# A two-block transformer step on one core: order of work in the mixture's first batch, at the seam between mixture and scan, and in SP's queue

## The chip, the cores and the metric

The kernel runs on one core of a Trainium2 chip. The metric is the device time of one execution in microseconds. Engines: TensorE (PE; its loads of stationary data are PEld), VectorE (DVE), ScalarE (ACT), GpSimd (POOL) and SyncE (SP), which issues most DMA transfers.

## The reference, cut to what matters

Two blocks, each with a token mixer and a feed-forward part, on x of shape (2, 2048, 256). The change touches the feed-forward part of the first block (a soft mixture of experts) and the mixer of the second (a state-space scan).

```python
# block 0, feed-forward: soft mixture, e=8 experts with t=128 slots each
logits = einsum('bsd,etd->bset', xn, se)
dispatch = softmax(logits, axis=1)                 # over the tokens
slots = einsum('bsd,bset->betd', xn, dispatch)
processed = gelu(slots @ w1) @ w2
combine = softmax(logits.reshape(b, s, e*t), -1)   # over the slots
x = x + gb * einsum('bnd,bsn->bsd', processed, combine)
# block 1, mixer: state space, 8 heads
h = layernorm(x) * (1 + ca) + sa
zxbcdt = layer_norm(h) @ W_in + b_in               # z, xs, B, C, dt
h_t = exp(dt*A) * h_(t-1) + (dt*xs) (x) B ;  y_t = h_t . C_t + D*xs
x = x + ga * (h + (y * silu(z)) @ W_out + b_out)
```

## The kernel before, in words

Each engine has a queue of its own, written out by hand, and waits on semaphores. `soft_mixture` and `state_space` are two such programs, one after the other; between them all engines meet at a barrier and the semaphores are cleared (`recycle`).

**The mixture** treats the batches b = 0 and 1 one after the other. `raw[e]` keeps the logits of expert e for 2048 tokens (128 slots x 2048). The combining softmax needs each token's largest logit. `spread_tops` sends these maxima through DRAM and back to all partitions (`top`). Then VectorE subtracts them (`shift`, L1268, 128x2048), ScalarE takes the exponential in place (`weights`, L1614), and TensorE multiplies with the experts' outputs (`combine`, L1846). The outputs are made by `outputs(b, et)` on TensorE: in batch 0 it takes 24 products of 128x256 an expert (three products of split operands for each of 8 parts, L61 to L63) into one of two PSUM banks, `pO[:, et % 2]`. `processed(b, e)` (VectorE, L1272) multiplies the result with the gate and frees the bank; `outputs` of expert et waits for `processed` of et - 2. The experts go in two halves of ES = 4. Between them TensorE makes `hidden(b, 1, j)`, ScalarE `gelu` (L1610) and the rounded `hidden_high` (L1586), and VectorE `hidden_low` (L1195). ScalarE has two `weights` ahead of the second half's `gelu`s and six behind them. `last_vector` is seven small VectorE operations on row statistics.

VectorE's order at the end of batch 0: for e in 0..3 `shift(e)`, `processed(e)`; then `shift(4)`, two `hidden_low`, `shift(5)`, six `hidden_low`, `shift(6)`, `shift(7)`; `last_vector`; `processed(4)` to `processed(7)`; then `modulate` for batch 1 and the loop of 16 `update(t)` behind `combine(t)`.

**The seam.** While batch 1 is combined, pairs of row tiles (PAIRS = 8 in each batch) are already normalised for the scan: `state_rows`, `state_offset` (VectorE), `state_normed`, `state_turned` (ScalarE), `state_turn`, `state_steps` (TensorE), `step_sizes` (VectorE, L1341), `turned_out` (SP, L1031). A pair's residual is x += ga * (h + b_out), three operations of 128x512. GpSimd makes these for most pairs (L1132 to L1136), VectorE for the last three of batch 1 (`residual`, L1423 to L1429), at the very end of its queue, ahead of the last `step_sizes`.

**The scan** has 32 steps n (batch n % 2, tile n // 2). Step n on TensorE: `project(n + 1)` (18 products of 128x384; the second third waits for `gate_bias`), `turn_y(n - 1)`, `states(n)`, `state_rows(n + 1)`, `within(n)`, `correlate(n + 1)`, `outputs(n - 1)`. ScalarE: `high`, `evacuate(n + 1)`, `y_high(n - 1)`, `by_state(n + 1)`, `decay(n + 1)`: eight Relus of 128x128 (L2234), then the copy of the next projection's bias into PSUM (`gate_bias`, L2217), then an exponential (L2239). VectorE: `weigh(n)` (L2358), `low(n + 2)`, `initial(n)` (L2363, L2365), `y_low(n - 1)` (L2369), `update(n)` (L2376), `gates(n + 1)` (L2347), `sums(n)` (L2382), `masked(n + 1)` (L2352), `finish(n - 1)` (L2387). GpSimd: `products` (L2144, L2146), `add_skip`, `skip` (with `dskip`), `gate`. `gate_bias(n)` writes the bank that `gates(n - 1)` reads, so it waits for it.

SP sends what a step needs just ahead (`stage(n)`: `cs`, `etot` and the 512 KB of `cumb`, L2098 to L2100), each `stage` once step n - 2 has read the buffers. The last 14 tiles' decays are made in the scan's first steps (`late_ratio`, `late_sizes`, `late_cumulate`, `late_sums`, `late_kept`, `late_turned`) and go through DRAM; `stage(5)` waits for that. `inputs(k)` loads a quarter of the projections' input (1024 KB). `m.wg`, `m.wu` and `m.wd` are weights that are first read at step 23.

## Time and profile before

| | |
|---|---|
| timed runs (3) | median 1670.1 us, 1668.47 to 1670.71 |
| profiled execution | 1671.12 us, its span 1669.4 us |
| granted TensorE clock over the span | 0.985 of full speed |
| busy: TensorE, VectorE, ScalarE, GpSimd | 1580.2 (95%), 1187.8 (71%), 776.2 (46%), 575.1 (34%) us |
| the mixture's batch 0 tail | about 497 to 541 us |
| seam between mixture and scan | about 866 to 871 us |
| scan | 871 to about 1200 us |

The span runs from the first to the last instruction. A busy share says how long an engine worked, not what held the end back; for that one reads, in each stretch, which wait ends last. The granted clock is that of TensorE alone: 1.00 is 2.4 GHz, 0.50 is 1.2 GHz.

### The profile page before, as it was taken

To read this page: it belongs to the slowest core of one execution; us is meant where nothing else is said; L and a number is where in the kernel's file an instruction comes from. 1 tells how busy PE (TensorE), PEld (TensorE's weight loads), DVE (VectorE), ACT (ScalarE), POOL (GpSimd) and SP (SyncE) were. 2 spreads that over 40 slices of the span, in tenths; PEclk is the share of its full clock that TensorE was granted. 3 is DMA by queue.
4 is the path that set the end of the run, shared out by engine and by line. 5 is a ranking of instruction groups with operands and counts; after the bars stand their busy time and mean duration, and the time that the engine had idled before them with its cause. 6 is when DMAs were issued, how large, how long until landed. Compare 5 with 4: busy or idle time off the path is not lost. (4 is left out here: it accounts for less than half of the span.)

```text
span 1669.4 us, 25600 instructions
## 1 busy us (share of the span) xinstructions
PE 1580.2 (95%) x9192; PEld 1365.4 (82%) x9192; DVE 1187.8 (71%) x2656; ACT 776.2 (46%) x1554; POOL 575.1 (34%) x474
## 2 busy tenths in 40 slices
PE   6899989999998999999979999999899999999996
PEld 4689878988888888867867889988688778888895
DVE  6877688864467756656877899989777736666763
ACT  3333333353356134427247778778411315444542
POOL 2100020000000003320536778877400024777764
PEclk9999999999999999999989999999899999999999
DMA  7000000010021000222025322322142135565643
GB/s 233 5 1 1 1 1 1 1 51 1 1 67 36 9 5 19 79 71 84 28 72 185 86 79 81 95 81 79 65 140 63 39 87 158 137 175 137 159 109 38
DMA packets 80886, 115.28 MB, mean 69 GB/s; under 512 B 15693, under 2 KB 60281, under 8 KB 80121
## 3 DMA queue, kind: packets, MB, share of 16 engines
q1 hardware_dynamic: 66808, 95.16, 17.9%
q0 software_dynamic: 12288, 17.31, 5.8%
q8 instruction: 74, 1.21, 0.3%
q10 hardware_dynamic: 1664, 1.18, 0.2%
q14 instruction: 52, 0.42, 0.1%
HBM read 85.32 MB, written 27.68 MB: 68 GB/s over the span
## 5 line engine op out<-in xcount | busy, mean ns | idle before, releaser
L2015 POOL DMA_INDIRECT k_xe<-rows_dram,idx x64 | 82.4, 1288 | 179.4 <-DVE idx L3087 141.1
L3154 POOL DMA_INDIRECT out<-k_eo,idx x64 | 117.0, 1828 | 74.5 <-DVE k_eo L3250 57.3
L1846 PE MATMUL d_pO<-d_sp,d_raw 128*128 128x257 f32 x512 | 114.6, 380 | 3.3 <-DVE x L1280 3.2
L1846 PEld LDWEIGHTS d_pO<-d_sp,d_raw 128*128 128x128 f32 x512 | 95.6, 189 | 17.7 <-DVE x L1280 4.1
L576 ACT ACTIVATE b_p<-b_pS,b_nmax 128x384 f32<-128x384 f32 (+16 forms) x32 | 38.1, 1192 | 131.7 <-DVE b_nmax L718 131.7
L61 PE MATMUL b_pO<-b_vh,b_ph 128*128 128x256 f32 x302 | 87.6, 290 | 7.3 <-DVE b_pl L699 7.2
L62 PE MATMUL b_pO<-b_vh,b_pl 128*128 128x256 f32 x302 | 85.3, 283 | 0.0
L63 PE MATMUL b_pO<-b_vl,b_ph 128*128 128x256 f32 x302 | 85.3, 283 | 0.0
L366 POOL TENSOR_TENSOR x<-x,b_vrow 128x256 f32<-128x256 f32 x32 | 24.1, 785 | 168.5 <-DVE b_hs L645 168.4
L2234 ACT ACTIVATE g_dlm<-d_cumb,mod 128x128 f32<-128x128 f32 x256 | 78.6, 400 | 2.0 <-DMA d_cumb<-cum_dram 2.0
L3209 ACT ACTIVATE k_act_g<-k_pg 128x512 f32<-128x512 f32 x64 | 38.3, 598 | 87.2 <-PE k_pu L63 87.0
L3267 DVE TENSOR_TENSOR k_hid<-k_act_g,k_pu 128x512 f32<-128x512 f32 x64 | 44.0, 687 | 42.8 <-ACT k_act_g L3209 42.2
L1599 ACT COPY d_raw<-pL 128x512 f32<-128x512 f32 x64 | 37.4, 587 | 79.6 <-PE pL L63 79.6
L61 PE MATMUL k_po<-k_wh,k_hh 128*128 128x256 f32 x256 | 72.4, 283 | 0.6 <-issue 0.6
L63 PE MATMUL k_po<-k_wl,k_hh 128*128 128x256 f32 x256 | 72.5, 283 | 0.0
L62 PE MATMUL k_po<-k_wh,k_hl 128*128 128x256 f32 x256 | 72.4, 283 | 0.0
L2845 ACT ACTIVATE i_act_g<-i_pg 128x512 f32<-128x512 f32 x30 | 17.9, 598 | 114.7 <-PE i_pu L63 114.7
L69 PE MATMUL pL<-d_winh,g_uh 128*128 128x384 f32 x186 | 65.1, 350 | 3.4 <-ACT pL L2217 2.6
L61 PE MATMUL b_pS<-b_kh,b_qh 128*128 128x512 f32 (+5 forms) x172 | 65.6, 381 | 1.4 <-DVE b_vl L691 1.4
L61 PEld LDWEIGHTS b_pO<-b_vh,b_ph 128*128 128x128 f32 x302 | 57.6, 191 | 10.8 <-DVE b_pl L699 10.5
L699 DVE TENSOR_TENSOR b_pl<-b_pT,b_ph 128x512 fp32r<-128x512 f32 (+3 forms) x86 | 49.9, 617 | 23.2 <-ACT b_ph L566 23.2
L1147 POOL MEMSET d_sp<- 128x4 f32 x4 | 0.3, 105 | 189.8 <-PE pL L63 165.8
(570 smaller groups left out, 5432.2 us busy)
## 6 DMA issues: line engine op xcount, KB each, us to landing
d_cumb<-cum_dram SPq DMA_DIRECT2D x32, 512.0 KB, 4.3
k_wf<-in_WgT SPq DMA_DIRECT2D x16, 512.0 KB, 4.1
k_wf<-in_WuT SPq DMA_DIRECT2D x16, 512.0 KB, 5.1
k_wf<-in_WdT SPq DMA_DIRECT2D x16, 512.0 KB, 6.7
rows_dram<-h_hx SPq DMA_DIRECT2D x32, 136.0 KB, 3.9
x<-in_x SPq DMA_DIRECT2D x8, 512.0 KB, 9.8
d_w<-in_w SPq DMA_DIRECT2D x4, 1024.0 KB, 6.2
uT_dram<-d_ug SPq DMA_DIRECT2D x16, 256.0 KB, 2.4
```

Of the source, the lines that this page charges most:

```text
L61: nc.tensor.matmul(out, ah, bh, start=start, stop=False)
L62: nc.tensor.matmul(out, al, bh, start=False, stop=False)
L63: return nc.tensor.matmul(out, ah, bl, start=False, stop=stop)
L69: nc.tensor.matmul(out, ah, bh, start=False, stop=False, skip_group_check=True)
L576: nc.scalar.activation(pr[:, n % 2, off:w], pS[:, a + off:a + w], ACT.Exp, bias=nmax[:, n % 2:n % 2 + 1], scale=scale, accum_out=esum[:, n ...
L699: nc.vector.tensor_tensor(pl[:, r, 0:w], src[:, 0:w], ph[:, r, 0:w].bitcast(F32), ALU.subtract).then_inc(s["lo_done"], 1)
L1846: last = nc.tensor.matmul(pO[:, t % 2, 0:PW], raw[e][:, t * P:(t + 1) * P], proc[e], start=e == 0, stop=e == E - 1)
L2015: nc.gpsimd.indirect_dma_start(out=m.xe[:, e % 2, t, :], out_offset=None, in_=m.rows, in_offset=bass.IndirectOffsetOnAxis(ap=column(m, e, ...
L2234: nc.scalar.activation(le[:, b, h, :], cumb[:, b, h, :], ACT.Relu, bias=cs[:, b, 3, h:h + 1], scale=-1.0).then_inc(s["dd_done"], 1)
L3154: nc.gpsimd.indirect_dma_start(out=out, out_offset=bass.IndirectOffsetOnAxis(ap=column(m, e, t), axis=0), in_=eo[:, e % 2, t, :], in_offse ...
L3209: nc.scalar.activation(act_g[:, f % 2], pg[:, f % 2], ACT.Gelu).then_inc(s["gelu_done"], 1)
L3267: nc.vector.tensor_tensor(hid[:, f % 2], act_g[:, f % 2], pu[:, f % 2], ALU.mult).then_inc(s["hid_done"], 1)
```

## The change

1. **Mixture, batch 0:** VectorE gates an expert's output (`processed`) ahead of that expert's subtraction (`shift`) for e < 4; of the second half, `last_vector` and `processed(0, 4)` come ahead of the last subtraction. Batch 1 keeps its order.
2. **Residuals:** those of the last two pairs leave the mixture's end and are made by VectorE in the scan (`last_residual`), one pair ahead of `masked(0)`, one behind `weigh(0)`. For this, batch 1's `uh` and `un` swap places, and `dskip` is allocated later. `initial(n)` for n < 2, `y_low(0)` and `finish` wait for these residuals.
3. **Second bias part:** in `decay(n)` for n < 3 the copy `gate_bias(n + 1)` comes ahead of the eight Relus, and `gates` of steps 1 and 2 behind `weigh` instead of behind `update`.
4. **SP's queue:** `stage(1)` ahead of all inputs, `stage(2)` and `stage(3)` ahead of `inputs(1)` and `inputs(3)`, and the three weights' transfers behind `stage(4)`.

```diff
@@ -925,9 +925,12 @@
         hid_low = placed("hid_low", [P, HT, 512], work_at, FR)
         PAIRS = NTB // 2
         spare = [m.x_at + NTB * C * 4, work_at]
-        uh_, un, ug, umod, ubout = [[nc.alloc_sbuf_tensor_at(f"d_{n}{b}", shape, F32, offset=spare[b] + o) for b in range(B)]
-                                    for n, shape, o in (("uh", [P, 2, 2, C], 0), ("un", [P, 2, 2, C], 4 * 4 * C), ("ug", [P, 2, CH, 2 * P], 8 * 4 * C),
-                                                        ("umod", [P, 3, C], 12 * 4 * C), ("ubout", [P, C], 15 * 4 * C))]
+        two_pairs = [P, 2, 2, C]
+        uh_, un, ug, umod, ubout = [[nc.alloc_sbuf_tensor_at(f"d_{n}{b}", shape, F32, offset=spare[b] + o[b] * 4 * C) for b in range(B)]
+                                    for n, shape, o in (("uh", two_pairs, (0, 4)), ("un", two_pairs, (4, 0)), ("ug", [P, 2, CH, 2 * P], (8, 8)),
+                                                        ("umod", [P, 3, C], (12, 12)), ("ubout", [P, C], (15, 15)))]
+        m.last_rows = [uh_[1][:, q % 2] for q in range(PAIRS - 2, PAIRS)]
+        m.last_gate, m.last_bout = umod[1][:, GA], ubout[1]
         token_tops = eT[0][0:NTB, 0:P]
         third = placed("uh_third", [P, 2, C], area + 10 * KB)
         rows_of = lambda b, q: third[:] if b and q == PAIRS - 3 else uh_[b][:, q % 2]
@@ -1484,15 +1487,19 @@
                     row_tops(b, 1)
                     keep_tops(b)
                 for e in range(ES):
+                    if not b:
+                        processed(b, e)
                     shift(b, e)
-                    processed(b, e)
+                    if b:
+                        processed(b, e)
                 for e in range(ES, E):
+                    if not b and e == E - 1:
+                        last_vector()
+                        processed(b, ES)
                     shift(b, e)
                     if not b and e < ES + 2:
                         for j in (range(2), range(2, HT))[e - ES]:
                             hidden_low(1, j)
-                if b + 1 < B:
-                    last_vector()
                 if b:
                     for k in range(CH):
                         input_low(k)
@@ -1500,7 +1507,7 @@
                         output_gated(k)
                     step_sizes(0, PAIRS - 2)
                     step_sizes(0, PAIRS - 1)
-                for e in range(ES, E):
+                for e in range(ES if b else ES + 1, E):
                     processed(b, e)
                 ahead = b + 1 < B
                 if ahead:
@@ -1548,9 +1555,8 @@
             step_sizes(1, PAIRS - 3)
             state_offset(1, PAIRS - 1)
             step_sizes(1, PAIRS - 2)
-            for q in range(PAIRS - 3, PAIRS):
-                for i in range(3):
-                    residual(q, i)
+            for i in range(3):
+                residual(PAIRS - 3, i)
             step_sizes(1, PAIRS - 1)
 
         @block.scalar
@@ -2020,7 +2026,6 @@
     with ExitStack() as ctx:
         sb, ps, sem = setup(nc, ctx)
         winh, winl, wogh, wogl, cumb = m.winh, m.winl, m.wogh, m.wogl, m.cumb
-        dskip = sb("g_dskip", [P, HEADS])
         uh, ul = m.uh, sb("g_ul", [P, B, CH, P], FR)
         cs, et = m.csb, m.etb
         spare = m.mod[:, :, SA:CA + 1, :].rearrange("p b m c -> p b (m c)")
@@ -2035,6 +2040,7 @@
         le, mt = m.dlm[:, 0:B], m.dlm[:, B]
         H = sb("g_H", [P, B, INNER])
         yh, yl = sb("g_yh", [P, INNER // P, P], FR), sb("g_yl", [P, INNER // P, P], FR)
+        dskip = sb("g_dskip", [P, HEADS])
         slabs = [m.pL[:, at:at + SLAB] for at in SLAB_AT]
         pbc, pz, pbt = m.pL[:, BC_AT:Z_AT], m.pL[:, Z_AT:X_AT], m.pL[:, 3 * GW:4 * GW]
         px = ((slice(0, P), m.pL[:, X_AT:X_AT + P]), (slice(P, INNER), slabs[2]))
@@ -2057,7 +2063,7 @@
                  "zr_done zeroed dd_done le_done m_done dtx_done xw_done xD_done i_ready st_ready y_ready "
                  "t1_done t2_done added hs_done h_done yg_done yT_ready yh_done yl_done o_ready x_done uh_done ul_done "
                  "gate_in shared_in gate_done stats mv_done ve_done powed scaled normed hT_ready hT_copied "
-                 "lg_ready mn_done ex_done rc_done sc_done bt2_done s_ready s_copied "
+                 "lg_ready mn_done ex_done rc_done sc_done bt2_done s_ready s_copied last_rows "
                  "a_in mods_in f_exp f_neg f_u f_chain f_log f_dA f_cum f_sums f_kept f_turned f_cumT f_out").split()
         s = {n: sem("g_" + n) for n in names}
         u_in = [sem(f"g_u_in{k}") for k in range(2 * B)]
@@ -2070,6 +2076,7 @@
         NJ = NTB * B
         LAST = NJ + 8
         SPLITS = (25, 27, 29)
+        PRIMED = 3
         tile = lambda n: n % B * NTB + n // B
         turned = lambda n: m.uT[:, :, tile(n) * P:(tile(n) + 1) * P] if n >= B else m.u0[:, n]
         is_job = lambda n: 0 <= n < NJ
@@ -2107,20 +2114,20 @@
                 sp.dma_start(m.rows.rearrange("(t p) c -> p t c", p=P)[:, tile(r), :],
                              hx[:, r % HB]).then_inc(m.rows_late if late_row else rows_out[r % HB], 16)
 
+            stage(1)
             inputs(0)
-            stage(1)
             inputs(2)
             sp.dma_start(gw[:], w["gate_wT"].rearrange("(h p) n -> p h n", p=P)).then_inc(s["gate_in"], 16)
-            for dst, src in ((m.wg, w["Ws_gT"]), (m.wu, w["Ws_uT"]), (m.wd, w["Ws_dT"])):
-                sp.dma_start(dst[:], src.rearrange("(h p) n -> p h n", p=P)).then_inc(s["shared_in"], 16)
+            stage(2)
+            stage(3)
             inputs(1)
             inputs(3)
-            stage(2)
-            stage(3)
             sp.wait_ge(s["f_chain"], 9)
             sp.dma_start(m.mod[:, :, SB:GB + 1, :].rearrange("p b m c -> p b (m c)"),
                          m.mod_dram[1][:, SB:GB + 1, :].rearrange("b m c -> b (m c)").partition_broadcast(P)).then_inc(s["mods_in"], 16)
             stage(4)
+            for dst, src in ((m.wg, w["Ws_gT"]), (m.wu, w["Ws_uT"]), (m.wd, w["Ws_dT"])):
+                sp.dma_start(dst[:], src.rearrange("(h p) n -> p h n", p=P)).then_inc(s["shared_in"], 16)
             sp.wait_ge(s["f_cumT"], 1)
             sp.dma_start(m.cum_dram[late.start * HEADS:late.stop * HEADS, :], cumT[0:NL, :]).then_inc(s["f_out"], 16)
             for n in range(5, LAST):
@@ -2228,12 +2235,14 @@
 
             def decay(n):
                 b = n % B
+                if n < PRIMED:
+                    gate_bias(n + 1)
                 act.wait_ge(cs_in[b], staged(n))
                 act.wait_ge(s["m_done"], max(n - 1, 0))
                 for h in range(HEADS):
                     nc.scalar.activation(le[:, b, h, :], cumb[:, b, h, :], ACT.Relu, bias=cs[:, b, 3, h:h + 1],
                                          scale=-1.0).then_inc(s["dd_done"], 1)
-                if is_job(n + 1):
+                if n >= PRIMED and is_job(n + 1):
                     gate_bias(n + 1)
                 act.wait_ge(s["dd_done"], (n + 1) * HEADS)
                 nc.scalar.activation(le[:, b], le[:, b], ACT.Exp, scale=-1.0).then_inc(s["le_done"], 1)
@@ -2360,12 +2369,26 @@
             def initial(n):
                 b = n % B
                 dve.wait_ge(s["i_ready"], n + 1)
+                if n < B:
+                    dve.wait_ge(s["last_rows"], 6)
                 nc.vector.tensor_tensor(heads(y[:, b]), heads(pi[:]), wide(cs[:, b, 2]), ALU.mult).then_inc(s["t1_done"], 1)
                 dve.wait_ge(s["h_done"], n)
                 nc.vector.tensor_tensor(heads(H[0:STATE, b]), heads(H[0:STATE, b]), wide(et[:, b], STATE), ALU.mult).then_inc(s["hs_done"], 1)
 
+            def last_residual(i):
+
+                tiles = slice(NT - 4 + 2 * i, NT - 2 + 2 * i)
+                h, xq = m.last_rows[i], m.x[:, tiles, :]
+                nc.vector.tensor_tensor(h, h, over(m.last_bout[:], 2), ALU.add).then_inc(s["last_rows"], 1)
+                dve.wait_ge(s["last_rows"], 3 * i + 1)
+                nc.vector.tensor_tensor(h, h, over(m.last_gate, 2), ALU.mult).then_inc(s["last_rows"], 1)
+                dve.wait_ge(s["last_rows"], 3 * i + 2)
+                nc.vector.tensor_tensor(xq, xq, h, ALU.add).then_inc(s["last_rows"], 1)
+
             def y_low(n):
                 dve.wait_ge(s["yh_done"], n + 1)
+                if n == 0:
+                    dve.wait_ge(s["last_rows"], 6)
                 nc.vector.tensor_tensor(yl[:].rearrange("p k t -> p (k t)"), pyT[:],
                                         yh[:].rearrange("p k t -> p (k t)").bitcast(F32), ALU.subtract).then_inc(s["yl_done"], 1)
 
@@ -2384,6 +2407,7 @@
             def finish(n):
                 xt = m.x[:, tile(n), :]
                 dve.wait_ge(s["o_ready"], n + 1)
+                dve.wait_ge(s["last_rows"], 6)
                 nc.vector.tensor_tensor(xt, xt, po, ALU.add).then_inc(s["x_done"], 1)
                 dve.wait_ge(s["x_done"], n + 1)
                 nc.vector.bn_stats(m.st[:, tile(n), :], xt).then_inc(s["stats"], 1)
@@ -2508,12 +2532,17 @@
             nc.vector.memset(H[:], 0.0)
             gates(0)
             nc.vector.memset(by_tile, 0.0)
+            last_residual(0)
             masked(0)
             for n in range(LAST):
                 if is_job(n - 2):
                     variance(n - 2)
                 if is_job(n):
                     weigh(n)
+                if n == 0:
+                    last_residual(1)
+                if n < PRIMED - 1:
+                    gates(n + 1)
                 if n % B and is_job(n - 7):
                     keep_scores((n - 7) // B)
                 if is_job(n + 2):
@@ -2530,7 +2559,7 @@
                     y_low(n - 1)
                 if is_job(n):
                     update(n)
-                if is_job(n + 1):
+                if n >= PRIMED - 1 and is_job(n + 1):
                     gates(n + 1)
                 if is_job(n):
                     sums(n)
```

## Rows read from the trace of the kernel before

**Rows 1.** By stretch: us, each engine's busy us, TensorE's granted clock, DMA share, GB/s.
```profile
861.00:880.00 19.00, 10.59 (x42) 9.27 (x43) 10.16 (x18) 9.08 (x25) 3.04 (x3) 0.55 0.47 141
880.00:1185.00 305.00, 297.27 (x1962) 261.11 (x1960) 268.72 (x576) 239.94 (x673) 235.22 (x188) 1.00 0.32 94
```

**Rows 2.** Timeline of VectorE in the mixture's first batch: start us, us, what.
```profile
502.70 2.29 DVE L1268 TENSOR_TENSOR d_raw<-d_raw,d_top 128x2048 f32<-128x2048 f32 x1 [3.57 <-DMA d_top<-tops_dram]
504.91 0.42 DVE L1272 TENSOR_TENSOR d_sp<-d_pO,mod 128x256 f32<-128x256 f32 x1
...
524.23 4.49 DVE L1268 TENSOR_TENSOR d_raw<-d_raw,d_top 128x2048 f32<-128x2048 f32 x2
```

**Rows 3.** Timeline of TensorE there; in brackets the idle us before and its releaser.
```profile
496.96 0.28 PE L61 MATMUL d_pO<-d_w2h,d_hid_high 128*128 128x256 f32 x1
...
502.50 0.28 PE L63 MATMUL d_pO<-d_w2l,d_hid_high 128*128 128x256 f32 x1
...
505.38 0.38 PE L61 MATMUL d_pO<-d_w2h,d_hid_high 128*128 128x256 f32 x1 [2.60 <-DVE d_sp L1272]
...
529.97 0.38 PE L61 MATMUL d_pO<-d_w2h,d_hid_high 128*128 128x256 f32 x1 [2.03 <-DVE d_sp L1272]
...
532.18 0.41 PE L61 MATMUL d_pO<-d_w2h,d_hid_high 128*128 128x256 f32 x1
...
537.30 9.07 PE L1846 MATMUL d_pO<-d_sp,d_raw 128*128 128x257 f32 x41
```

**Rows 4.** Timeline of ScalarE there.
```profile
512.80 0.60 ACT L1610 ACTIVATE d_work<-pL 128x512 f32<-128x512 f32 x1
...
524.90 10.93 ACT L1614 ACTIVATE d_raw<-d_raw 128x2048 f32<-128x2048 f32 x6
```

**Rows 5.** Timeline of all engines where mixture and scan meet; last, the landing of `uT_dram`'s transfers.
```profile
864.12 0.51 SPq L1031 DMA_DIRECT2D uT_dram<-d_ug  x1
...
864.24 1.85 PE L1864 MATMUL d_pT<-mod,d_ug 128*128 128x8 f32 x8 [1.21 <-ACT d_ug L1636]
864.46 0.69 DVE L1423 TENSOR_TENSOR d_uh<-d_uh,d_ubout 128x512 f32<-128x512 f32 x1
...
870.62 0.27 DVE L2336 MEMSET mod<- 128x256 f32 x1 [1.88 <-PEq L50]
...
DMA to landing us min/median/max: 2.4/2.5/12.9
```

**Rows 6.** Timeline of TensorE in the scan's first steps.
```profile
875.99 0.80 PE L2591 MATMUL pL<-g_bcT 128*128 128x128 f32 x2 [0.95 <-ACT pL L2217]
...
886.88 0.44 PE L69 MATMUL pL<-d_winh,g_uh 128*128 128x384 f32 x1 [1.66 <-ACT pL L2217]
...
897.03 0.44 PE L69 MATMUL pL<-d_winh,g_uh 128*128 128x384 f32 x1 [0.91 <-ACT pL L2217]
```

**Rows 7.** Timeline of ScalarE there.
```profile
886.02 0.80 ACT L2217 COPY pL<-d_bias 128x768 f32<-128x768 f32 x1 [0.80 <-DVE g_wide L2347]
...
893.83 2.45 ACT L2234 ACTIVATE g_dlm<-d_cumb,mod 128x128 f32<-128x128 f32 x8 [1.77 <-DMA d_cumb<-cum_dram]
```

**Rows 8.** Timeline of VectorE there.
```profile
876.82 0.29 DVE L2352 TENSOR_TENSOR mod<-pL,d_upto 128x128 f32<-128x128 f32 x1 [3.56 <-PE pL L2591]
...
882.91 0.57 DVE L2342 TENSOR_TENSOR g_ul<-uT,g_uh 128x256 fp32r<-128x256 f32 x1 [4.47 <-ACT g_uh L2197]
...
889.84 1.22 DVE L2358 TENSOR_TENSOR g_dlm<-g_dlm,mod 128x1024 f32<-128x1024 f32 x1
```

**Rows 9.** Issue of stage(2), GpSimd's wait for stage(5), and the page's line of such transfers.
```profile
884.82 0.50 SPq L2098 DMA_DIRECT2D mod<-d_cs  x1
...
924.12 1.04 POOL L2144 TENSOR_TENSOR g_wide<-g_wide,mod 128x512 f32<-128x512 f32 x1 [3.75 <-issue]
...
d_cumb<-cum_dram SPq DMA_DIRECT2D x32, 512.0 KB, 4.3
```

**Rows 10.** GpSimd's second product of a step, by line: ns min/median/max.
```profile
L2146 POOL TENSOR_TENSOR g_wide<-g_wide,mod x32: 1039/1226/1582, 874.7 to 1175.9; 128x512 f32<-128x512 f32 x32
```

## The prediction

> **What bounds the kernel now.** I read the page first, then the busy time by stretch, then each engine in order of time where the change edits it. The page puts TensorE far ahead of the other engines, and by stretch it is busy 297 of 305 us in the scan after its start [rows 1]. So a microsecond counts if TensorE stands still in it, or works in it at the low clock. In order of time the places are three.
>
> (a) The first batch's tail in the mixture. TensorE waits 2.60 us before 505.38 and 2.03 us before 529.97, both times for VectorE's gating `processed` [rows 3]. From 531.4 to 534.7 its granted clock is 1.2 instead of 2.4 GHz: the 128x256 product lasts 0.41 us instead of 0.28, and the 48 products of the last two outputs take 7.33 us, to 537.30, while the 48 of the first two took 5.66, from 496.96 to 502.62 [rows 3].
>
> (b) The end of the mixture. TensorE ends at 866.09, VectorE at 868.74, the scan's first instruction is at 870.5 [rows 5].
>
> (c) The first four steps of the scan, where TensorE waits 0.95, 1.66 and 0.91 us for ScalarE's bias copy [rows 6]. TensorE is busy 10.6 us of 19 between 861 and 880, at 0.55 of its clock [rows 1]. So what the scan's start gains is kept, as long as no other engine becomes the bound.
>
> **Part 1, `processed` ahead of `shift` (first batch).** Nothing is added or removed; VectorE's order changes. Now: `shift(0,0)` waits for the maxima's transfer until 502.70 and lasts 2.29 us, and `processed(0,0)` stands behind it, though its product, the first 24 of those 48, ended at about 499.9 [rows 2, 3]. After: `processed(0,0)` (0.42 us) fits in VectorE's 3.57 us of idle time [rows 2]. The third output's accumulation starts at 502.62 instead of 505.38: 2.76 us. `processed(0,1)` still follows `shift(0,0)` and ends at 505.3, as TensorE ends its third accumulation at 505.45, so no wait comes back. The fourth ends at 508.3.
>
> ScalarE's GELUs of the second half start when the fourth output and the second exponential are done. The latter ends at 509.5, so the table load moves from 511.45 to 509.5 and the first GELU from 512.8 to 510.85. The eight pairs of GELU and rounding take 1.35 us each now, up to 523.6 (a table load of 1.28 us ahead of 524.90 [rows 4]), since they wait for TensorE; by themselves they take about 1.25, twice a GELU's 0.60 [rows 4] and a little; so they catch up, the last rounding ends at 520.9, and the last `hidden_low` at 521.8. TensorE needs it at 521.8: no wait, and 2.76 us stay.
>
> The second wait: two subtractions (4.49 us, to 528.7 [rows 2]), the seven small operations of `last_vector` (0.9 us) and only then `processed(0,4)` at 529.50. After: `shift(0,6)` 521.7 to 524.0, `last_vector` to 524.85, `processed(0,4)` to 525.25, against a TensorE that is ready at 525.0. 0.3 us are left of 2.1: 1.8 us saved. With 0.3 us of idle time instead of 2.6 and 2.1 us I take the slow stretch to go too: 7.33 - 5.66 = 1.67, of which I count 1.6. It follows the two waits, and between 30 and 860 us of the span there is no second one.
>
> Next late: the combination of tile 0 needs all eight exponentials. ScalarE has six to do, 10.93 us [rows 4], after a table load of 1.28: 520.9 + 1.3 + 10.9 = 533.1. TensorE reaches the combination at 531.1 instead of 537.30 and its last expert at 531.1 + 14 x 0.22 = 534.2 (the row has 9.07 us for 41 products [rows 3]). It is hidden by 1.1 us. Sum of part 1: 2.76 + 1.8 + 1.6 = 6.2 us. Bounds: 4.6 with the slow stretch kept, 6.5 with the rest of the wait gone. Everything to 861 is released by this work, in its order, so it moves along.
>
> **Part 2, two pairs' residuals out of the mixture's end.** Six additions and products of 0.69 us leave VectorE's queue [rows 5]. After the third pair's three (to 864.5) the last `step_sizes` waits for TensorE's 866.09 [rows 5] and ends at 866.3. The block waits for SP too: its last `turned_out`, issued at 864.12, lands 2.4 to 2.5 us later [rows 5], at 866.6. VectorE's first instruction of the scan, at 870.62, stands 1.88 us behind its last of the mixture [rows 5], and I keep these: 868.5, 2.1 us sooner. Bounds: 2.4 (the transfer hidden), 1.5 (it lands 0.6 us later).
>
> The six operations come back in the scan, 2.1 us each time. `last_residual(0)` lies in VectorE's 3.56 us of idle time before 876.82, `last_residual(1)` in the 4.47 us before 882.91 [rows 8]. Without that cover each would cost 2.1 us. What the later waits on them guard (`initial(0)`, `y_low(0)`, `finish`) starts later by itself. GpSimd works beside the first three. Its product L2146 lasts from 1.04 to 1.58 us, by what runs beside it [rows 10]; three such are 1.6 us late at most, done by 878.4, and TensorE takes them at 880. (The Trainium skill, GPSIMD Engine Reference, section Specifications, says that VectorE's instructions with two inputs in SBUF contend with GpSimd for its SBUF interface. These six are such instructions, so the rule speaks against the move; by it and by row alike the price is hidden, and the sum stays.)
>
> **Part 3, bias copy and `gates` sooner for the first three steps.** In coordinates of before, ahead of part 2's shift. The copy of step 1 goes ahead of the eight Relus (2.45 us [rows 7]): the 0.95 us wait goes [rows 6], the exponential behind it is 0.5 us later, needed only at 881. At step 2 the copy at 886.02 waited for `gates(1)` behind the state's update [rows 7]; `gates(1)` now comes behind `last_residual(1)`, at 881.5, the copy at 881.8. The 1.66 us go too; TensorE is 2.6 us ahead.
>
> Here VectorE gives some back: the eight operations of `late_ratio` stand ahead of the weighting at 889.84 [rows 8], which moves by 1.15 only, and `gates(2)` (0.6 us) now stands ahead of `y_low(0)`. TensorE waits for both; it is 0.7 us ahead at its first output product.
>
> At step 3 the 0.91 us [rows 6] go, and ScalarE's 1.77 us wait for the decays [rows 7] as well, by part 4: 3.1 us ahead at project(4). The late decays bind next. Their sums come 1.9 us sooner, their turned copy 2.3; the transfer and stage(5) hang on it, and GpSimd has waited 3.75 us for stage(5) before 924.12 [rows 9]. From there 2.3 us remain, which I take. Bounds: 0.7 (the lowest point on the way) and 3.5 (all three waits).
>
> **Part 4, order of SP's queue.** stage(2), issued from 884.82 [rows 9], stood behind 4 MB of projections' input and 1.5 MB of weights, and ScalarE saw it at 893.83 [rows 7]; the median of such a transfer is 4.3 us [rows 9]. Ahead of half of the input it is there at about 889. Moved back: inputs(1) and inputs(3), first read by step 16; the three weights, first read at step 23. They will be issued from 893 to 905, 3.5 MB. Before, 5.5 MB took no more than the 22.4 us from 871.4 to 893.8, so 3.5 MB take no more than 14: they are there ahead of stage(5) at 916 and stand beside stage(4) alone, which has 5 us to spare. Where that cover is missing a stage costs what stage(2) lost, 3.5 to 4 us. stage(1) ahead of inputs(0) delays these by 1.9 us, to about 880, read at 881: nothing. The shift of `dskip` and of the buffers changes addresses only.
>
> **Sum.** 6.2 + 2.1 + 2.3 = 10.6 us. The profiled execution took 1671.1 us (span 1669.4): 1660.5 after, span 1658.8. The three timed runs have 1670.1 as median, 1 us less: 1659.5. No change can be told from one within 0.2%, 3.3 us.
>
> **Rivals.**
> - *The slow stretch stays or moves.* For: TensorE's clock also falls at 862 behind idle times of 1.2 us only. Against: none of the scan's waits up to 1.7 us is followed by it. 6.2 becomes 4.6: 1661.1. Chance 0.15. (The Trainium skill, TensorE: Matmul & The Clock Gate, Part 1, says that the activity monitor's window runs freely, so that the same kernel sees other slow stretches from run to run. By that rule the 1.5 us may turn up elsewhere; one profile can't show it.)
> - *VectorE becomes the scan's bound.* It is busy 269 of the 305 us [rows 1], and then part 3 is lost: 8.3 saved, 1661.8. Against: TensorE's 297. Chance 0.14.
> - *Part 1 does little, ScalarE's exponentials decide.* If they run till 535.8 as now, TensorE is held at tile 0 from 534.2 on: 1.6 us less, 9.0 saved, 1661.1; if the last subtraction, now behind `processed(0,4)`, keeps them back by its 2.29 us too, 3.9 less, 1663.4. Against: their start hangs on TensorE's fourth output. Chance 0.10.
> - *A stage is late behind the moved transfers*, 4 us: 6.6 saved, 1663.5. Chance 0.07.
> - *Slower.* The clock comes back later in the scan. It is at 1.2 GHz from 862 to 879.5, though TensorE works from 872.8 on but for the 0.95 us [rows 1, 6]. Each microsecond of TensorE's work at that clock costs half of one, so from 21 us more of it, up to 901, it eats the 10.6; at 30 us it would be 1674.5. Against: TensorE gets fewer idle times there. Chance 0.03; to it comes 0.01 for the rest.
>
> My forecast has 0.50. The likeliest case's own range is 1657.4 to 1661.7. With the rivals up to 1663.5, scatter of about 1 us and two later slow stretches (near 1205 and 1375) that may be cut differently by 1 to 2 us: 1656.5 to 1664.5. Faster by over 0.2%: 0.93, within: 0.04, slower: 0.03.
>
> **What the profile after would show.** No wait over 0.5 us of TensorE on L1272 in 500 to 531; the combination's start at about 531.2; 128x256 products at 0.28 us up to it. The scan's first instruction 8.2 us sooner (862.3). No ScalarE wait for `d_cumb` at step 2, the bias copies of steps 1 to 3 ahead of the Relus, TensorE's waits for L2217 gone. The scan's end 10.6 us sooner, and the same lead up to the last scatter. I am wrong if the lead at 540 (old time) is not near 6, or if it shrinks between 930 and 1185.

## The result, and the profile after

The changed kernel took 1660.03 us (median of 4 runs, 1659.04 to 1660.9), the kernel before 1670.4 beside it (4 runs, 1668.47 to 1672.5): ratio 0.9937, 95% interval 0.9920 to 0.9955. The span went from 1669.4 to 1658.6 us; 1658.8 was forecast. The total was right to 0.5 us. The terms were less so, as the trace shows. Of the executions of one kernel some are 5 us or more apart, so the small gains below are read from the traces, stretch by stretch.

**The mixture's tail.** VectorE of the changed kernel, first batch (against [rows 2]):

```profile
500.79 0.42 DVE L1275 TENSOR_TENSOR d_sp<-d_pO,mod 128x256 f32<-128x256 f32 x1 [0.85 <-PE d_pO L63]
503.70 2.29 DVE L1271 TENSOR_TENSOR d_raw<-d_raw,d_top 128x2048 f32<-128x2048 f32 x1 [2.49 <-DMA d_top<-tops_dram]
...
525.72 0.18 DVE L101 SCALAR_TENSOR_TENSOR rstd<-tmp,rstd 128x16 f32<-128x16 f32 x1
525.81 0.42 DVE L1275 TENSOR_TENSOR d_sp<-d_pO,mod 128x256 f32<-128x256 f32 x1
526.14 2.28 DVE L1271 TENSOR_TENSOR d_raw<-d_raw,d_top 128x2048 f32<-128x2048 f32 x1
```

Gating now stands inside the wait for the maxima's transfer, and the fifth gating ahead of the last subtraction. TensorE (against [rows 3]) has no wait listed between 500 and 532, and its 128x256 products stay at 0.28 us up to the combination (0.38 for one at the head of a group, as before); ScalarE (against [rows 4]) is 0.8 to 1 us behind the forecast and not the bound:

```profile
531.99 0.28 PE L63 MATMUL d_pO<-d_w2l,d_hid_high 128*128 128x256 f32 x1
532.11 1.25 PE L1852 MATMUL d_pO<-d_sp,d_raw 128*128 128x257 f32 x5
```

```profile
511.80 0.60 ACT L1616 ACTIVATE d_work<-pL 128x512 f32<-128x512 f32 x1
...
523.01 10.92 ACT L1620 ACTIVATE d_raw<-d_raw 128x2048 f32<-128x2048 f32 x6
```

**The seam** (against [rows 5]), timeline of TensorE, then of VectorE:

```profile
858.85 1.84 PE L1870 MATMUL d_pT<-mod,d_ug 128*128 128x8 f32 x8 [1.21 <-ACT d_ug L1642]
```

```profile
858.64 0.69 DVE L1432 TENSOR_TENSOR x<-x,d_uh_third 128x512 f32<-128x512 f32 x1
860.73 0.17 DVE L1344 TENSOR_TENSOR mod<-d_pT,mod 128x16 f32<-128x16 f32 x1 [1.40 <-PE d_pT L1870]
863.23 0.27 DVE L2345 MEMSET mod<- 128x256 f32 x1 [2.33 <-PEq L50]
```

From the start of TensorE's last group to the scan's first VectorE instruction it is 4.38 us; before, 870.62 - 864.24 = 6.38. SP's last `turned_out` lands at 861.15, 2.08 us ahead of the scan's first VectorE instruction. VectorE had ended at 860.91, and 1.88 us behind that would have been 862.79; so the transfer now ends the stage.

**The scan's start.** VectorE (against [rows 8]), TensorE (against [rows 6]), ScalarE (against [rows 7]):

```profile
865.79 0.63 DVE L2382 TENSOR_TENSOR d_uh<-d_uh,d_ubout 128x512 f32<-128x512 f32 x1
866.45 1.41 DVE L2384 TENSOR_TENSOR d_uh<-d_uh,d_umod 128x512 f32<-128x512 f32 x1
867.90 1.42 DVE L2386 TENSOR_TENSOR x<-x,d_uh 128x512 f32<-128x512 f32 x1
...
871.22 0.68 DVE L2382 TENSOR_TENSOR d_uh<-d_uh,d_ubout 128x512 f32<-128x512 f32 x1
871.94 1.42 DVE L2384 TENSOR_TENSOR d_uh<-d_uh,d_umod 128x512 f32<-128x512 f32 x1
873.39 1.42 DVE L2386 TENSOR_TENSOR x<-x,d_uh 128x512 f32<-128x512 f32 x1
874.72 0.67 DVE L2356 SCALAR_TENSOR_TENSOR g_wide<-g_wide,pL 128x512 f32<-128x512 f32 x1
875.32 0.41 DVE L2351 TENSOR_TENSOR g_ul<-uT,g_uh 128x256 fp32r<-128x256 f32 x1
```

```profile
875.79 0.44 PE L69 MATMUL pL<-d_winh,g_uh 128*128 128x384 f32 x1 [1.44 <-DVE g_ul L2351]
880.39 0.66 PE L2626 MATMUL g_pyT<-ident,g_wide 128*128 128x128 f32 x4 [1.21 <-POOL g_wide L2169]
883.36 2.00 PE L2650 MATMUL g_py<-g_wide,g_dlm 128*128 128x64 f32 x16 [0.38 <-DVE g_dlm L2367]
886.59 0.38 PE L61 MATMUL g_pyT<-d_wogh,g_yh 128*128 128x256 f32 x1 [0.95 <-DVE g_yl L2392]
```

```profile
883.93 0.80 ACT L2224 COPY pL<-d_bias 128x768 f32<-128x768 f32 x1 [0.54 <-DVE g_wide L2356]
884.67 2.45 ACT L2243 ACTIVATE g_dlm<-d_cumb,mod 128x128 f32<-128x128 f32 x8
```

The bias copy stands ahead of the Relus, these don't wait for their row any more, and no wait of TensorE names the copy of the second bias part. But four other waits, 3.98 us, stand where three of 3.52 stood [rows 6]. The last pair's three operations end at 874.8, 11.6 us behind the scan's first VectorE instruction, with `gates(1)` and `low(2)` queued behind them, and four of the six last 1.41 or 1.42 us, not the 0.69 that they took in the mixture. GpSimd works on its products in these microseconds:

```profile
867.28 1.49 POOL L2153 TENSOR_TENSOR g_wide<-g_wide,mod 128x512 f32<-128x512 f32 x1
868.73 1.49 POOL L2158 TENSOR_TENSOR g_wide<-g_wide,g_dskip 128x512 f32<-128x512 f32 x1
871.33 1.47 POOL L2151 TENSOR_TENSOR g_wide<-g_wide,mod 128x512 f32<-128x512 f32 x1 [1.11 <-ACT g_wide L2213]
872.77 1.49 POOL L2153 TENSOR_TENSOR g_wide<-g_wide,mod 128x512 f32<-128x512 f32 x1
```

The busy time by stretch (against [rows 1]) shows the low clock, which lasts here from 858.2 to 868.5 (10.2 us), where it was from 862.5 to 879.6 (17.1 us):

```profile
858.00:869.00 11.00, 6.15 (x23) 5.71 (x24) 6.96 (x11) 6.44 (x19) 2.85 (x3) 0.53 0.28 83
869.00:1176.00 307.00, 297.92 (x1969) 261.48 (x1967) 276.12 (x582) 241.27 (x678) 238.68 (x189) 1.00 0.33 99
```

**All kernels by stretch.** Each number is the difference of two starts in the kernel's own profiled execution: T, SP's issue of the first batch's `tops_dram` (496.48 before, 497.27 after; what comes ahead of it is the same code, and differs by how the clock's slow stretches fall); C, the first `d_pO<-d_sp,d_raw` on TensorE; E, TensorE's last `d_pT<-mod,d_ug`; S, the scan's first VectorE instruction; then VectorE's `x<-x,g_pyT` of the scan's steps 5 and 31, and the span's end (the last column to 0.05 us).

| kernel | T to C | C to E | E to S | S to 5 | 5 to 31 | 31 to end |
|---|---|---|---|---|---|---|
| before | 40.82 | 326.94 | 6.38 | 76.36 | 247.85 | 474.57 |
| after | 34.84 | 326.74 | 4.38 | 75.38 | 247.14 | 472.85 |
| mixture alone | 34.25 | 326.18 | 6.55 | 76.05 | 247.85 | 472.82 |
| gate first | 36.74 | 327.82 | 6.56 | 76.12 | 247.88 | 472.81 |
| last shift later | 36.98 | 326.80 | 6.50 | 76.16 | 247.83 | 473.96 |
| without mixture | 40.45 | 326.74 | 4.38 | 74.96 | 247.12 | 472.72 |
| residuals alone | 40.42 | 328.56 | 4.38 | 77.94 | 247.10 | 472.88 |
| no early bias | 34.60 | 327.43 | 4.39 | 75.78 | 247.10 | 472.52 |
| old queue | 34.62 | 326.74 | 4.39 | 77.63 | 247.13 | 474.14 |
| placement | 42.31 | 327.14 | 6.13 | 76.34 | 247.10 | 472.28 |
| residuals, one column | 34.43 | 327.17 | 4.39 | 74.34 | 247.11 | 470.94 |
| a pair in each gap | 34.47 | 327.42 | 4.54 | 74.01 | 247.09 | 473.99 |
| both pairs back | 34.59 | 326.23 | 6.59 | 73.84 | 247.09 | 472.92 |
| gaps, no early bias | 34.55 | 328.74 | 4.53 | 75.92 | 247.11 | 474.01 |

The change by stretch: -5.98, -0.20, -2.00, -0.98, -0.71, -1.72, and +0.79 ahead of T: -10.8 us.

Every row is one execution. How far two executions of the same code differ is seen down the columns. S to 5 takes 76.05 to 76.36 in the five kernels whose scan starts as before, and 75.38 and 74.96 in the two that start it as the changed kernel does. So in that column 0.4 us can't be told from nothing, and the change's part there is 0.7 to 1.4 us. T to C takes 34.25 to 34.84 in all eight kernels with the mixture's part. The clock is no rival for the scan's start: in those five kernels the low clock lasts to 9.0, 9.7, 10.5, 9.1 and 8.7 us behind S (in the order of the table), and the longer it lasts the shorter S to 5 is, if anything; in the two it lasts to 5.2 and 7.9, and the one with more of it is the shorter.

The kernels executed once took 1666.51 (gate first), 1665.6 (last shift later), 1659.85 (no early bias), 1663.83 (old queue), 1670.51 (placement), 1656.67 (residuals, one column), 1659.49 (both pairs back) and 1663.23 us (gaps, no early bias). Single executions of the kernel before spread over 11 us, so nothing is concluded from these times.

### The profile page after: what moved, and what is told of

It reads as the page before. It is cut to its first block and busy times, and to the rows that moved or that the text cites. A ratio compares the mean times of both kernels' runs of the same rounds, so it can differ in the third digit from the quotient of the medians.

```text
span 1658.6 us, 25635 instructions
## 1 busy us (share of the span) xinstructions
PE 1573.0 (95%) x9192; PEld 1360.2 (82%) x9192; DVE 1192.8 (72%) x2656; ACT 775.7 (47%) x1554; POOL 578.0 (35%) x474
## 3 DMA queue, kind: packets, MB, share of 16 engines
q8 instruction: 74, 1.21, 0.3%
## 5 line engine op out<-in xcount | busy, mean ns | idle before, releaser
L63 PE MATMUL k_po<-k_wl,k_hh 128*128 128x256 f32 x256 | 72.5, 283 | 0.0
L61 PEld LDWEIGHTS b_pO<-b_vh,b_ph 128*128 128x128 f32 x302 | 57.9, 192 | 10.2 <-DVE b_pl L699 9.8
```

What stands on the lines that cost most here:

```text
L61: nc.tensor.matmul(out, ah, bh, start=start, stop=False)
L63: return nc.tensor.matmul(out, ah, bl, start=False, stop=stop)
```

## The experiments

**1. The mixture's part alone** (the kernel before with it):

```diff
+                    if not b:
+                        processed(b, e)
                     shift(b, e)
-                    processed(b, e)
+                    if b:
+                        processed(b, e)
                 for e in range(ES, E):
+                    if not b and e == E - 1:
+                        last_vector()
+                        processed(b, ES)
                     shift(b, e)
...
-                if b + 1 < B:
-                    last_vector()
...
-                for e in range(ES, E):
+                for e in range(ES if b else ES + 1, E):
                     processed(b, e)
```

> The kernel before, with the order of VectorE's work in the first batch's mixture changed and nothing else. My theory: the two waits of TensorE for the first outputs go, and with them the slow-clock stretch at 531 to 535, so the first combination starts 6 us sooner against the start of that part (5 to 6.2), and nothing later gives it back: span 6 us shorter, ratio 0.9964 (0.9958 to 0.9970). The two parts of the change are independent, so this and the kernel without the mixture's part add up to the whole, 10.4 us. Rival A: a slow-clock stretch goes with the order of the scan's start and not with the mixture, and some comes or goes elsewhere when all is 6 us sooner: the combination is 6 us sooner but the span only 2.6 or as much as 9.4 us shorter (3.4 us, one stretch as the traces show it, either way). Rival B: the stretch at 531 to 535 goes only because the whole program is shifted, not because the waits go: it stays here, and the combination is 4.4 to 4.6 us sooner.

1663.44 us against 1671.61 (medians): ratio on record 0.9961 (0.9948 to 0.9974), 6.5 us; the medians themselves are 8.2 us apart, within the interval. The combination starts 6.57 us sooner from T, and from C to step 31 nothing is given back. By the profiles the span is 9.2 us shorter, near rival A's 9.4, since 1.8 us more lie behind the scan, where the low clock lasts 3.4 us in place of 13.7; the timed runs' 6.5 us don't bear that out as this part's gain. Rival B falls, and not in this kernel alone: all four kernels with the old order in the whole of the tail have a stretch of low clock there (it starts at 506 or at 530 to 534, in the kernel with changed placement at both), and none of the ten with one or both waits gone has any.

**2 and 3. Its halves.** The first is the loop over four experts, the second the two calls ahead of the last shift.

> The kernel before, with only the gating of the four first experts ahead of the subtraction of maxima; last_vector and the fifth gating stay where they were. My theory: the wait for the first gated output, 2.76 us, goes and the wait behind the fifth, 1.8 us, stays, since the last shift and last_vector still stand ahead of it: combination 2.8 us sooner if the slow stretch needs that second wait, 4.4 if the first wait alone had brought it. Rival: the exponentials on ScalarE, which start behind the shifts, are now what the tail ends on, and the combination is less than 1.5 us sooner.

> The kernel before, with only last_vector and the fifth gating ahead of the last shift. My theory: the second wait, 1.8 us, goes, the first, 2.76 us, stays; the combination is 1.8 us sooner, and 3.4 us if the slow stretch is the second wait's alone. Together with the other half, the two make the 6.0 us of the whole to within 0.5 us, if waits and stretch are all that there is. Rival: ScalarE's last group of exponentials, which now starts later by the gating's length, holds the combination, and this half is worth 1 us or less.

Gate first: 4.08 us sooner; TensorE's other wait stands:

```profile
527.84 0.39 PE L61 MATMUL d_pO<-d_w2h,d_hid_high 128*128 128x256 f32 x1 [2.12 <-DVE d_sp L1272]
533.61 2.56 PE L1849 MATMUL d_pO<-d_sp,d_raw 128*128 128x257 f32 x11
```

Last shift later: 3.84 us sooner, and the first wait stands:

```profile
504.53 0.39 PE L61 MATMUL d_pO<-d_w2h,d_hid_high 128*128 128x256 f32 x1 [2.56 <-DVE d_sp L1272]
```

Neither has the slow stretch near 531 to 535. Each half is worth its wait and the stretch: they add up to 7.92, the whole to 5.98 or 6.57, and the excess of 1.35 to 1.94 fits the stretch counted twice, at 1.67 worked out from its 48 products. Each of the two cases, 4.4 and 3.4, was named; that both hold, and the halves so miss their expected sum of 6.0 by 1.9, was not expected. Both rivals, that ScalarE holds the combination, fall. With gating first alone, two stretches of 3.4 us at the low clock turn up later, ahead of the scan, at 721 and 827, where before had none; C to E is 327.82 and not 326.94. The first of them, in a window of 4 us:

```profile
721.00:725.00 4.00, 4.00 (x10) 1.87 (x9) 3.15 (x10) 0.19 (x1) 0.71 (x1) 0.57 0.71 238
```

So something like the first rival's case, that the stretch moves, did occur, though in another kernel than the one forecast. Whether these are the stretch moved or others isn't shown: other kernels have such stretches at 718 to 834 too, two of them (residuals alone, placement) besides one in the tail.

**4. The change without the mixture's part** (edit 1 taken back).

> The changed kernel with the mixture's order of before: only the residuals, the second bias part and the transfers are changed. My theory: the seam gives 2.0 us and the start of the scan 1 us, as the trace of the whole change shows, and the rest is the clock's: step 5 of the scan 3.0 us sooner, step 31 some 3 to 3.8 us sooner. Span 3 to 4 us shorter if the shorter slow stretch behind the scan (3.4 us in place of 13.7) belongs to the mixture's part, 5 us if it belongs to this one: ratio 0.9979 or 0.9970. Rival: the seam's 2.0 us were there only because the mixture's end was shifted against the chip's clock; then step 5 is 1 us sooner and the ratio 0.9990.

1664.8 us: ratio on record 0.9967 (0.9957 to 0.9978), 5.5 us. E to S 4.38 as with the whole change: the seam's gain needs nothing of the mixture. From S to step 5 it takes 74.96, and 247.12 from there to step 31; from E on step 5 comes 3.4 us sooner, and the rival's 1 us falls. The two parts' times add up to 12.0 us against 10.4 for the whole, within the intervals. By stretch, from T to step 31, they add up to 12.2 us against 9.9: 0.96 more from T to C, 0.76 from C to E and 0.73 from S to 5, where kernels with equal code differ by up to 0.6, 0.8 and 0.4. That the parts are independent is shown no better than that. 31 to end is 472.7 here and 472.8 in experiments 1 and 2, so what the change seemed to gain behind the scan can be put down to neither part.

**5. The residuals alone** (parts 1, 3 and 4 of the change taken back).

> The kernel before, with only the last two pairs' residuals moved into the scan (their buffers' new places with them): mixture, bias parts and SP's queue as before. My theory: the seam gives 2.0 us, since TensorE, VectorE and SP meet sooner at the mixture's end, but in the scan the six operations at 1.4 us beside GpSimd's stand ahead of masked(0), gates(1) and low(2) with nothing to pay for them: scan's start to its step 5 takes 76.4 us as before or up to 2 us more, so the seam's gain is kept whole or nearly lost. With the scan's other two parts the same stretch takes 75.2. Rival: VectorE's idle time (3.56 and 4.47 us) hides them even so, step 5 is 2 us sooner against the mixture's end, and the other two parts are worth the whole 1.0 to 1.4 us.

1668.93 against 1671.0: ratio 0.9985 (0.9969 to 1.0001), not told from the kernel before. The seam's 2.0 us are there. S to 5 is 77.94, with a slow stretch from 906 to 910 that before hasn't, worth 1.7 us at most: -0.1 to 1.6 us longer than before. Up to that stretch nothing is late: TensorE starts the 16 products `within(2)` 31.66 us behind S, and 31.70 before. So here VectorE's idle time does hide the residuals, as the rival says and as the prediction had it; that the other two parts are then worth the whole of the start's gain, as the rival goes on, isn't shown by this. The trace has the same operations beside GpSimd and without it, since here GpSimd's next product starts only at 882.01:

```profile
874.30 1.46 DVE L2378 TENSOR_TENSOR d_uh<-d_uh,d_umod 128x512 f32<-128x512 f32 x1
875.79 1.42 DVE L2380 TENSOR_TENSOR x<-x,d_uh 128x512 f32<-128x512 f32 x1
...
879.83 0.69 DVE L2378 TENSOR_TENSOR d_uh<-d_uh,d_umod 128x512 f32<-128x512 f32 x1
880.56 0.69 DVE L2380 TENSOR_TENSOR x<-x,d_uh 128x512 f32<-128x512 f32 x1
```

```profile
875.17 1.49 POOL L2149 TENSOR_TENSOR g_wide<-g_wide,mod 128x512 f32<-128x512 f32 x1
876.62 1.49 POOL L2154 TENSOR_TENSOR g_wide<-g_wide,g_dskip 128x512 f32<-128x512 f32 x1
882.01 1.04 POOL L2147 TENSOR_TENSOR g_wide<-g_wide,mod 128x512 f32<-128x512 f32 x1 [3.90 <-ACT g_wide L2209]
```

Twice the time on VectorE, and 1.49 for 1.04 on GpSimd. Only the last pair's operations differ: they come ahead of GpSimd's product here and beside it in the changed kernel, where the early bias brings that product from 10.9 us behind S to 8.1. Experiment 6 confirms that it is the early bias: without it the product is at 10.9 us in the changed kernel too, and the last pair's operations take 0.68 and 0.69 us.

**6. The changed kernel without early bias:**

```diff
-                if n < PRIMED:
-                    gate_bias(n + 1)
...
-                if n >= PRIMED and is_job(n + 1):
+                if is_job(n + 1):
                     gate_bias(n + 1)
...
-                if n < PRIMED - 1:
-                    gates(n + 1)
...
-                if n >= PRIMED - 1 and is_job(n + 1):
+                if is_job(n + 1):
                     gates(n + 1)
```

> The changed kernel, with gates and the second bias part at their old places in every step (behind the decays on ScalarE, behind update on VectorE); residuals and SP's queue as changed. My theory: TensorE waits for the bias copy in steps 1 to 3 again (0.95, 1.66 and 0.91 us before), but what the changed kernel has in their place, 1.44 us for g_ul, 1.21 for g_wide and 0.38 for g_dlm, in part goes, since gates no longer stands ahead of low: from the scan's start to step 5 it takes 75.4 to 76.4 us, that is 0 to 1 us more than the changed kernel. Rival: early bias is worth its three waits, 3.5 us, and the stretch takes 78 us or more. Other rival: it costs, and the stretch is under 75.

S to 5 takes 75.78, 0.40 longer, as expected, and no more than two kernels with the same start differ by. Both rivals fall. Part 3 was forecast to bring nearly all of the start's 2.3 us.

**7. The changed kernel with SP's order of before.**

> The changed kernel with SP's transfers at the scan's start in the order of before. My theory: step 2's decays wait 1.8 us for their row on ScalarE as before, and of that 0.3 to 1 us reaches TensorE: scan's start to step 5 takes 75.7 to 76.4 us in place of 75.4. Rival: step 2's waits hide behind the scan's VectorE, nothing changes (within 0.1 us). Other rival: the transfers are the whole of the gain, and it takes 77.4.

S to 5 takes 77.63, 2.25 longer; a slow stretch from 899 to 903 has at most 1.7 of it. ScalarE waits for its row again, and GpSimd, whose products wait for the same `stage(2)`, idles 6.69 us where it idles 2.02 in the changed kernel. TensorE's longest wait is for GpSimd:

```profile
886.48 2.46 ACT L2243 ACTIVATE g_dlm<-d_cumb,mod 128x128 f32<-128x128 f32 x8 [2.19 <-DMA d_cumb<-cum_dram]
```

```profile
886.58 1.04 POOL L2151 TENSOR_TENSOR g_wide<-g_wide,mod 128x512 f32<-128x512 f32 x1 [6.69 <-issue]
```

```profile
892.16 0.66 PE L2626 MATMUL g_pyT<-ident,g_wide 128*128 128x128 f32 x4 [1.71 <-POOL g_wide L2169]
```

Worth 0.55 to 2.25 us by these bounds. Ahead of the slow stretch TensorE starts `within(2)` 31.49 us behind S against 30.38, so 1.1 us is already there. The rival without effect falls. The other, that the transfers are the whole of the gain (77.4), is not excluded: 1.1 us is about what the start gains in all, since the early bias and the last pair nearly cancel.

**8. Addresses alone** (the kernel before, `dskip` allocated behind `yh` and `yl`).

> The kernel before, with one tensor of 8 numbers a partition allocated behind two others, not ahead of them, as in the changed kernel: nothing is executed otherwise. The question is the 0.73 us that the scan from step 5 to 31 is shorter in both kernels with the changed placement (247.12 against 247.85 us in those without, each repeated to 0.03 us). My theory: addresses 32 bytes lower make a few operations shorter, and the stretch takes 247.1 here. Rival: it is the phase in which the engines enter the steady scan, set by the other order at its start; then it stays 247.85 here.

247.10: the place of `dskip` alone makes it, 0.75 us, whether by the tensors between, now 32 bytes lower, or by its own new address. The rival falls. Busy time by line in that stretch, with mean ns: before, then with the address changed.

```profile
L71 PE MATMUL pL<-d_winl,g_uh 128*128 128x384 f32 x144 | 49.0, 340 | 0.0
```

```profile
L71 PE MATMUL pL<-d_winl,g_uh 128*128 128x384 f32 x144 | 48.2, 334 | 0.0
```

These projections are the largest difference between the two. Neither of their operands (`winl` and `uh`) nor the PSUM that they write has moved, so it is not the address of what they touch; how an address does it stays open.

**9. The price of the residuals in the scan** (the additions and the product take only the first column of their other operand too):

```diff
-                h, xq = m.last_rows[i], m.x[:, tiles, :]
+                h, xq = m.last_rows[i][:, :, 0:1], m.x[:, tiles, 0:1]
```

> The changed kernel, with the six operations of the two moved residuals cut to the first of their 256 columns; the rest of those rows is left out. This prices the residuals in the scan's start. My theory: each full one takes 1.41 us beside GpSimd's products in place of 0.69, and the last pair's three stand ahead of gates(1) and low(2); without them TensorE's waits for g_ul (1.44), g_wide (1.21) and the low part of y (0.95) go or shrink, GpSimd's products there take 1.04 and not 1.49 us, and from the scan's start to its step 5 it takes 72.5 to 74.1 us in place of 75.4: the prediction's 2.3 us instead of 1.0. Rival: VectorE had the time and the waits come from GpSimd or ScalarE all the same; then it takes 75.0 or more.

S to 5 takes 74.34, 1.04 us less, between my range (72.5 to 74.1) and the rival's 75; neither has it. GpSimd's five products from 865 to 873 took 1.03 to 1.05 us, and TensorE's wait for `g_ul` is gone.

**10. A pair in each gap** (the changed kernel with the lines below, and its semaphore counts made to fit three operations in place of six):

```diff
+            for i in range(2):
+                residual(PAIRS - 2, i)
             step_sizes(1, PAIRS - 1)
+            residual(PAIRS - 2, 2)
...
-            last_residual(0)
+            last_residual(1)
             masked(0)
...
-                if n == 0:
-                    last_residual(1)
```

> The changed kernel, with one pair's residual in each of VectorE's gaps: the last but one in the mixture, two of its operations ahead of the last step sizes, where VectorE waits 1.40 us for TensorE, and one behind them, where it waits 2.33 us for the stage's end; the last pair ahead of masked(0), where the last but one stood; none behind weigh(0). My theory: the seam stays at 4.4 us, nothing stands ahead of gates(1) and low(2) any more, and the scan's start to step 5 takes 1 to 2 us less than the changed kernel's 75.4, about what the kernel with narrow residuals shows: span 1 to 2 us shorter, ratio to the kernel before 0.9928 (0.992 to 0.994). Rival: the gap in the mixture isn't free, since the step sizes come 0.3 to 1 us later and the transfer behind them too, and nothing is gained.

S to 5 takes 74.01, E to S 4.54: 1.21 us sooner than the changed kernel. In the mixture the three operations take 0.68 or 0.69 us each; VectorE now ends the stage by 0.15 us:

```profile
857.90 0.68 DVE L1426 TENSOR_TENSOR d_uh<-d_uh,d_ubout 128x512 f32<-128x512 f32 x1
858.62 0.69 DVE L1429 TENSOR_TENSOR d_uh<-d_uh,d_umod 128x512 f32<-128x512 f32 x1
859.75 0.17 DVE L1344 TENSOR_TENSOR mod<-d_pT,mod 128x16 f32<-128x16 f32 x1 [0.44 <-PE d_pT L1873]
859.85 0.68 DVE L1432 TENSOR_TENSOR x<-x,d_uh 128x512 f32<-128x512 f32 x1
862.41 0.27 DVE L2348 MEMSET mod<- 128x256 f32 x1 [1.88 <-PEq L50]
```

In the scan, where the changed kernel has the last pair (3.6 us from 871.22), VectorE has this much idle time left:

```profile
871.42 0.69 DVE L2359 SCALAR_TENSOR_TENSOR g_wide<-g_wide,pL 128x512 f32<-128x512 f32 x1 [0.95 <-ACT g_wide L2219]
872.81 0.48 DVE L2354 TENSOR_TENSOR g_ul<-uT,g_uh 128x256 fp32r<-128x256 f32 x1 [0.70 <-ACT g_uh L2207]
```

Timed: 1659.24 us (5 runs) against 1670.27, ratio 0.9935 (0.9922 to 0.9949; 0.992 to 0.994 was expected). That is faster than the kernel before; from the changed kernel's 0.9937 the times don't tell it apart. The gain rests on the traces, and against the kernel without the mixture's part, which starts the scan as the changed kernel does, it is 0.8 us and not 1.2.

**11 and 12. Both pairs in the mixture, the last behind the step sizes; a pair in each gap without early bias.**

> The changed kernel with both pairs' residuals in the mixture, the last three operations behind the last step sizes, so that SP's transfers don't wait for them but the stage's end does. My theory: VectorE ends the stage at 0.17 + 4 x 0.69 us behind TensorE, the seam is 6.0 to 6.2 us and not 4.4, as in the kernel before, and the scan's start to step 5 is as with narrow residuals: net 0 to 1 us worse than a pair in each gap. Rival: uncontended and out of the scan, the six are cheaper in sum, and the scan's step 5 comes sooner than with a pair in each gap.

> A pair in each gap, and gates and the second bias part at their old places. In the changed kernel putting them back cost 0.4 us or less. My theory: that was because the residuals stood in front of the early gates; with these away the early bias is worth its waits, and without it the scan's start to step 5 takes 1 to 2.5 us longer than with a pair in each gap. Rival: the early bias is worth under 0.5 us here too, VectorE's other work or the head rows' transfers set the start.

Both back: E to S 6.59 (6.0 to 6.2 expected), S to 5 73.84, together 1.88 us more than a pair in each gap, twice what I allowed; the rival falls. In S to 5 the first pair is thus worth 0.17 us (74.01 against 73.84). Without early bias: 75.92, 1.91 us more than with it. So the early bias is worth 1.9 us when no residual stands ahead of the second step's gates, and 0.4, within the scatter, when one does. In both comparisons the low clock also lasts longer without early bias, to 9.9 us behind S against 5.2, and to 10.5 against 6.2. By the kernels with equal code in the table its share is small; no run separates it.

## Why the prediction was right, and where it was not

- **Part 1, 6.2 forecast, 5.98 measured, 6.57 when alone.** Right in its steps: both waits went, the slow stretch went, ScalarE's exponentials stayed hidden. The prediction took the stretch to go with both waits; in experiments 2 and 3 it goes with either. On the span's own clock the lead is 5.2 us at 540, since the changed kernel's execution was 0.79 us late ahead of T; from step 5 to 31 it grows from 8.4 to 9.1 us.
- **Part 2, 2.1 forecast, 2.00 measured**, and by the mechanism named: VectorE now idles 2.33 us where it was 1.88, so it isn't what ends the stage; SP's last `turned_out`, issued at 858.73 and landed at 861.15, is. That idle time is the room that experiment 10 used.
- **"The six operations come back in the scan, 2.1 us each time", hidden.** This is the step that failed. It took 0.69 us from the mixture's rows, where GpSimd has nothing to do, and priced the contention on GpSimd's side alone. Beside GpSimd four of the six take 1.41 or 1.42 us. The first pair still fits into 3.56 us [rows 8]. The second would have been hidden in the 4.47 us of before, as experiments 5 and 6 show; with the early bias that gap is 0.95 + 0.70 = 1.65 us (experiment 10), and the same early bias brings GpSimd's product beside the pair. So 3.6 us stand where 1.65 are free, ahead of `gates(1)` and `low(2)`, and 1.0 to 1.4 us reach step 5 (74.01 against 74.96 and 75.38). An estimate from these numbers: without contention the pair's 2.1 us would have overrun the gap by 0.4 us and not by 1.9, so most of it is contention; no run has the early bias and the pair uncontended, so the two shares aren't shown. (The Trainium skill's GPSIMD Engine Reference, section Specifications, has VectorE's instructions with two SBUF inputs contend with GpSimd. The traces agree, and on both engines: 0.69 against 1.41 us, and 1.04 against 1.49.)
- **Parts 3 and 4, 2.3 forecast, 0.98 measured.** Their mechanisms hold, as the waits gone show, but the second pair takes most of part 3: 0.4 instead of 1.9. Part 4 had no term of its own: its 1.77 us of ScalarE's wait was part of the 2.3, and its path over GpSimd's products wasn't named; taking it back costs 0.55 to 2.25. With the pairs in the gaps the start gives 76.36 - 74.01 = 2.35 us, and start and seam together 82.74 - 78.55 = 4.19, against the 2.3 and 4.4 of the sum. That GpSimd's wait for `stage(5)` passes the gain on, as forecast, fits: it ends 0.94 us sooner behind S in the changed kernel, and 2.31 sooner with the pairs in the gaps.
- **"The shift of `dskip` and of the buffers changes addresses only."** True, but put at nothing without a reason: in every kernel that has `dskip`'s new place it is worth 0.71 to 0.76 us in the scan.
- **Behind the scan, 0 forecast, 1.72 in the profile.** Hardly the change's: the profile of before has the low clock for 13.7 us between 1200 and 1215, that of after for 3.4. The kernel that differs from before by an address alone is at 472.28, even lower. The prediction allowed 1 to 2 us for this.

So the sum came out by luck, because errors cancelled: 0.2 and 0.1 us too much for parts 1 and 2 and 1.3 for the scan's start, against 0.7 of address, 0.2 between C and E and 1.7 behind the scan, less 0.8 ahead of T, none of them counted. The terms that were forecast, 10.6 in sum, measured 8.96 us. The rival "VectorE becomes the scan's bound" (part 3 lost, 8.3 saved) was nearly right for the first steps and wrong for the rest.

## What to carry to other kernels

Price a moved instruction by who works beside it at its new place: these VectorE operations with two inputs in SBUF took twice their time beside GpSimd's, on the idle engine that was to hide them. Measure a gap as it is after all parts of the change, since one part may close the gap in which another was put. Compare two profiles by stretches between landmarks, so that what the clock gives or takes elsewhere is not booked to the change.

## What the runs showed of the hardware

- A 128x512 fp32 operation with both inputs in SBUF takes 0.69 us on VectorE with GpSimd idle, and 1.41 to 1.46 beside its products, which take 1.47 to 1.49 in place of 1.04. The sums fit taking turns (0.7 us of waiting and 0.7 of work), which is an inference. The first addition of each residual stayed at 0.63 to 0.68; each started ahead of GpSimd's product (865.79 against 866.15, 871.22 against 871.33), which fits it.
- An allocation of 32 bytes a partition ahead of other tensors cost the steady scan 0.75 us in 248, repeated to 0.05 us in 14 traces.
- Short stretches at a granted clock of 1.2 GHz, about 3.4 us each, come at other places in kernels that differ only elsewhere, among them 506, 721, 824, 899 and 906. Each costs up to 1.7 us (an estimate, half of its length), as much as this change's smaller parts. The runs of the kernel before spread from 1665.99 to 1676.84.
